# Attention and expert routing on one core: the order of a batch drawn up anew, long products halved, rank products joined, scatters one batch later

## What is computed

```python
# attention: 16 heads of width 8, all projected by U, V (8x8 here)
q, k, v = x @ Wq.T + bq, x @ Wk.T + bk, x @ Wv.T + bv       # per head, then @ V
att = softmax((q @ V) @ (k @ V).T / sqrt(rank))
y   = ((att @ (v @ V)) @ U.T) @ Wo.T + bo
x1  = layernorm(x + y)
# experts: 8 experts of hidden width 512, the best two per token
scores, idx = top_k(softmax(x1 @ gate_w.T), 2)              # scores normalised to sum 1
h   = relu(x1 @ w1[e].T + b1[e]);  out_e = h @ w2[e].T + b2[e]
out = layernorm(x1 + sum_e combine[e] * out_e)
```

## Time and profile before

| | us |
|---|---|
| median of 3 runs | 1183.03 (1179.2 to 1183.96) |
| the profiled execution | 1178.9 |
| its span in the trace | 1177.1 |
| PE / DVE / ACT / POOL busy | 1031.5 / 970.8 / 882.7 / 587.4 |
| first scores of batch 0, last scores of batch 15 | 63.9, 827.8 |
| first transpose of the second phase | 867.9 |

### The profile page before, as it was taken

One profiled execution on the slowest core, in us unless ns is written; L12 is line 12 of the kernel. 1 busy time (PEld: TensorE's weight loads), 2 busy tenths in 40 slices (PEclk: granted clock), 3 DMA queues, 4 the chain that ended last, 5 costly groups with the idle time before them and its releaser, 6 DMA issues. The chain is left out here.

```text
span 1177.1 us, 24412 instructions
## 1 busy us (share of the span) xinstructions
PE 1031.5 (88%) x7581; PEld 495.2 (42%) x7581; DVE 970.8 (82%) x2115; ACT 882.7 (75%) x1129; POOL 587.4 (50%) x823
## 2 busy tenths in 40 slices
PE   3578989999999999998999999897349999999967
PEld 1112223222222222222322222222249999999952
DVE  4778898999989989899899998991458888888845
ACT  1057878788788787887878878778259999999927
POOL 1223417346264372652734626314347777777745
PEclk9879999999999999999999999998669999999989
DMA  3633232241322423324224132200022222222246
GB/s 85 242 101 92 63 102 72 82 132 49 107 79 76 134 61 96 97 68 118 75 82 127 53 107 73 78 13 20 19 74 70 68 69 69 70 69 69 66 184 253
DMA packets 96420, 104.86 MB, mean 89 GB/s; under 512 B 21696, under 2 KB 73666, under 8 KB 96208
## 3 DMA queue, kind: packets, MB, share of 16 engines
q1 hardware_dynamic: 85872, 81.88, 24.0%
q0 software_dynamic: 8448, 16.93, 4.6%
q10 hardware_dynamic: 2016, 4.98, 1.2%
HBM read 56.06 MB, written 47.39 MB: 88 GB/s over the span
## 5 line engine op out<-in xcount | busy, mean ns | idle before, releaser
L753 DVE TENSOR_REDUCE row_max<-score_ps 128x2 f32<-128x1024 f32 x512 | 618.0, 1221 | 70.8 <-PE score_ps L552 68.1
L639 ACT ACTIVATE probs<-score_ps 128x1024 f32<-128x1024 f32 x512 | 521.3, 1022 | 134.2 <-PE score_ps L534 112.8
L800 POOL DMA_INDIRECT routed_d<-rows,slot_i x128 | 126.4, 988 | 318.7 <-DVE slot_i L722 272.2
L515 PE MATMUL av_ps<-probs,v_one 128*9 128x512 f32 x2048 | 271.0, 601 | 6.1 <-ACT probs L639 5.2
L552 PE MATMUL score_ps<-k_stack,q_stack 48*128 48x512 bf16 x1024 | 202.5, 392 | 54.7 <-ACT probs L639 26.4
L534 PE MATMUL score_ps<-q_stack,k_stack 51*128 51x512 bf16 x1024 | 201.4, 391 | 25.0 <-DVE row_max L753 20.8
L1058 ACT ACTIVATE w_cur<-experts 128x1156 f32 x136 | 158.4, 1167 | 38.0 <-issue 18.3
L534 PEld LDWEIGHTS score_ps<-q_stack,k_stack 51*128 51x128 bf16 x1024 | 49.2, 93 | 313.4 <-issue 161.2
L1154 POOL DMA_INDIRECT y_d<-y_out,place x136 | 136.8, 1006 | 44.8 <-issue 44.8
L1015 PE MATMUL up_ps<-xt_sb,w_cur 128*128 128x128 f32 x1088 | 145.5, 277 | 0.0
L1023 PE MATMUL down_ps<-w_cur,hidden_r 128*128 128x128 f32 x1088 | 143.4, 275 | 0.0
(11 more groups left out here) (171 smaller groups left out, 1050.8 us busy)
## 6 DMA issues: line engine op xcount, KB each, us to landing
k_stack<-k_stack_d SPq DMA_DIRECT2D x128, 96.0 KB, 2.5
q_stack<-q_stack_d SPq DMA_DIRECT2D x128, 96.0 KB, 2.6
x_rows_sb<-routed_d SPq DMA_DIRECT2D x136, 65.0 KB
q_stack_d<-q_parts SPq DMA_DIRECT2D x32, 192.0 KB
k_stack_d<-k_parts SPq DMA_DIRECT2D x30, 192.0 KB
experts<-expert_rows SPq DMA_DIRECT2D x1, 4624.0 KB, 15.1
x_t<-x_cols SPq DMA_DIRECT2D x16, 256.0 KB, 4.0
q_stack_d<-q_parts SPq DMA_DIRECT2D x32, 128.0 KB
```

The source lines that it names most:

```text
L515: last = nc.tensor.matmul(av_ps[32 * g:32 * g + V_COLS, :], v_one[n.parity][:, kb, HG * hg + g, :], probs[:, (2 * j + g // 2) % P_RING, g ...
L639: nc.scalar.activation(probs[:, s % P_RING, :, :], exp_bank(b, s)[:, :, :], ACT.Exp).then_inc(S["exp_done"], 1)
L753: nc.vector.tensor_reduce(row_max[:, m // (STEPS // 2), :, m % (STEPS // 2)], max_bank(b, s)[:, :, :], AX.X, ALU.max).then_inc(S["red_done ...
L800: nc.gpsimd.indirect_dma_start(routed_d, bass.IndirectOffsetOnAxis(ap=slot_i[n.parity][:, w, t:t + 1], axis=0), rows[n.parity][:, w, t, :] ...
```

## The change

- The pieces of `misc` get other steps. Before, every piece stands in an odd step. Now the y transposes stand at steps 14, 22, 0 (of the next batch) and 5, the rank at 24, the row maxima at 9 and 26, x1 at 28, the logits at 30.
- The long products are cut in two: q at steps 2 and 3 (before 13), k at 16 and 17 (before 15), the output product at 11 and 12 (before 11), v at 19 and 20 (before 19).
- The ranks come from 5 matmuls of 40, 32, 24, 16 and 8 columns instead of 14 of 8; `chosen_any` has a column block of zeros more.
- DVE gets one piece of `choose` a step (`CHOOSE_AT`), for batch b-2 and a batch later than before; `route` at 25 to 28; the sum, statistics and moments of the layer norm in three steps (13, 14, 16) instead of two.
- ACT's copies move to the steps behind their products; the scaling of x1 goes to steps 20, 22, 24, 26.
- POOL scatters batch b-3 in the body of b, two after every split; the last two batches' scatters come at the end. SP's order has q stores ahead of the second maxima rows, and `x_t` at the end of a body instead of the start of the next, which is the same place in its queue.

```diff
-SCALE_AT = 17
+SCALE_AT = (20, 22, 24, 26)
+CHOOSE_AT = (2, 3, 4, 5, 7, 8, 9, 10, 11, 12, 17, 18, 19, 20, 21, 22)
+ROUTE_AT = (25, 25, 26, 27, 28)
...
-                            if s == 13 and proj:
-                                pe.wait_ge(x_loaded[n2.parity], n2.count_parity(16, 16))
-                                emptied(s)
-                                nc.tensor.matmul(misc_ps[:, :], wq_t[:, :], x_t[n2.parity][:, :], start=True, stop=True).then_inc(S["q_done"], 1)
+                            if s in (2, 3) and proj:
+                                if s == 2:
+                                    pe.wait_ge(x_loaded[n2.parity], n2.count_parity(16, 16))
+                                    emptied(s)
+                                at = slice((s - 2) * T // 2, (s - 1) * T // 2)
+                                last = nc.tensor.matmul(misc_ps[:, at], wq_t[:, :], x_t[n2.parity][:, at], start=True, stop=True)
+                                if s == 3:
+                                    last.then_inc(S["q_done"], 1)
...
-                            if s == 17 and cur:
+                            if s == 14 and cur:
                                 emptied(s)
                                 y_transpose(b, 0)
...
-                            if s == 5 and prev2:
+                            if s == 24 and prev2:
                                 emptied(s)
                                 pe.wait_ge(S["top_step"], p2.count(TOP_STEPS, 13))
...
+                                counts = misc_ps[:, 0:(QT + 1) * E].rearrange("p (t e) -> p t e", e=E)
+                                nc.tensor.matmul(counts, before[:, :], chosen_any[p2.parity][:, :, :], start=True, stop=False)
+                                for k in range(QT):
+                                    last = nc.tensor.matmul(counts[:, k + 1:QT + 1, :], ones[:, :],
+                                                            chosen_any[p2.parity][:, k:k + 1, :].to_broadcast([P, QT - k, E]), start=False, stop=(k == QT - 1))
...
-                            if s <= 4 and prev2:
-                                for k in (2 * s + 6, 2 * s + 7):
-                                    choose(p2, k)
+                            if s in CHOOSE_AT and prev2:
+                                choose(p2, CHOOSE_AT.index(s))
...
+                        if nxt and n1.c + 2 < B:
+                            n3 = n1 + 2
+                            sp.wait_ge(S["v_done"], n1.count(1, 1))
+                            sp.dma_start(x_t[n3.parity][:, :], x_cols[n3.c, :, :]).then_inc(x_loaded[n3.parity], 16)
```

More of the change, by code:

```diff
@@ L172, in build_layer @@
             weight_sum = asb("weight_sum", [P, QT])
-            chosen_any = [asb(f"chosen_any{n}", [P, QT, E], bf16) for n in range(2)]
+            chosen_any = [asb(f"chosen_any{n}", [P, QT + 1, E], bf16) for n in range(2)]
             slot = asb("slot", [P, QT, E])
@@ L444, in misc @@
                                 max_transpose(1)
-                            if s == 11 and prev:
-                                pe.wait_ge(S["ynt_sb"], p1.count(1, 1))
-                                emptied(s)
-                                for t in range(QT):
+                            if s in (11, 12) and prev:
+                                if s == 11:
+                                    pe.wait_ge(S["ynt_sb"], p1.count(1, 1))
+                                    emptied(s)
+                                for t in (2 * s - 22, 2 * s - 21):
@@ new lines, in misc @@
+                            if s in (19, 20) and nxt:
+                                if s == 19:
+                                    pe.wait_ge(x_loaded[n1.parity], n1.count_parity(16, 16))
+                                    emptied(s)
+                                for t in (2 * s - 38, 2 * s - 37):
+                                    last = nc.tensor.matmul(misc_ps[:, t * P:(t + 1) * P], x_t[n1.parity][:, t * P:(t + 1) * P], wv_t[:, :], start=True, stop=True)
+                                if s == 20:
+                                    last.then_inc(S["v_done"], 1)
@@ L456, in misc @@
+                            if s == 22 and cur:
                                 emptied(s)
[L457 to L458 removed]
+                                y_transpose(b, 1)
+                            if s == 24 and prev2:
                                 emptied(s)
                                 pe.wait_ge(S["top_step"], p2.count(TOP_STEPS, 13))
[L461 to L468 removed]
@@ L469, in misc @@
-                            if s == 19 and nxt:
-                                pe.wait_ge(x_loaded[n1.parity], n1.count_parity(16, 16))
-                                emptied(s)
-                                for t in range(QT):
-                                    last = nc.tensor.matmul(misc_ps[:, t * P:(t + 1) * P], x_t[n1.parity][:, t * P:(t + 1) * P], wv_t[:, :], start=True, stop=True)
-                                last.then_inc(S["v_done"], 1)
-                            if s == 21 and cur:
-                                emptied(s)
-                                y_transpose(b, 1)
@@ L802, in scatter, with rows_ready @@
                                     rows[n.parity][:, w, t, :], None).then_inc(scattered[n.parity], 16)
[L804 to L807 removed]
+                        def rows_ready(n):
+                            pool.wait_ge(S["place_out"], n.count(1, 1))
+                            pool.wait_ge(S["top_step"], n.count(TOP_STEPS, TOP_STEPS))
+                            pool.wait_ge(S["slot_step"], n.count(SLOT_STEPS, SLOT_STEPS))
+                            pool.wait_ge(S["x1_ready"], n.count(QT, QT))
+                        if prev3 and cur:
+                            rows_ready(p3)
+                            scatter(p3, 0, 2)
                         if prev:
@@ L873, in stacks @@
                                                  stack_d[n.parity][a, :, :, pairs, :].rearrange("s r c t -> (s r) c t")).then_inc(stack_loaded[hg], 16)
-                        if cur and proj:
-                            sp.wait_ge(S["v_done"], b.count(1, 1))
-                            sp.dma_start(x_t[n2.parity][:, :], x_cols[n2.c, :, :]).then_inc(x_loaded[n2.parity], 16)
                         if nxt:
@@ L888, in body @@
                             store_parts(sp, q_stack_d[n2.parity], q_parts, Q_PLACES)
-                        if nxt and not cur:
-                            max_rows(n1, 0)
+                        if cur:
+                            max_rows(b, 1)
                         if proj and not is_first(b):
```

182 lines of the change are left out of this document (88 added, 94 removed).

## The result

The changed kernel takes **1301.7 us**, median of 4 runs (1296.42 to 1303.11). Beside it the kernel before took 1181.12 (4 runs, 1178.34 to 1183.96). The ratio is **1.1028**, 95% interval 1.1008 to 1.1048: slower by a tenth. The forecast was 1285 us, 1236 to 1330, and slower with a chance of 0.91.

A forecast was written before the change was run, and what follows sets the result against it. It took a loop of odd scores, exponential, even maxima and `av`, 2.81 us a pair, to bound the kernel. Terms summed to +101.6 on the profiled 1178.9, giving 1280.5, plus 4.1 for the median: 1285 us, range 1236 to 1330.

The forecast's parts named there:

- The rule: Pair costs 2.81 us, plus odd-step excess over 0.75, all PE work behind even `av`, 0.19 per last-moment ACT copy.
- A: PE products now behind `av` in even steps (transposes, half products, logits, row maxima, ranks) add their time: +88.9 us.
- B: ACT copies: v and x1 ahead of odd exponentials +5.7, three y copies beside PE products −8.2; together −2.5 us.
- C: The five long products lose their excess in odd steps: −22.7 us.
- D: DVE pieces, spread one a step, heal a leftover of 0.53 us in 14 batches: −7.4 us.
- E: PE's q product at step 2 waits 2.8 us for the load of `x_t` in 13 batches: +36.4 us.
- F: Maxima rows land late for the scores of step 16, 0.3 us in 13 batches: +3.9 us, bounds 0 and 9.
- G: Start: q product of batch 2 waits for `x_t` in batch 0, at lower clock: +3.5 us, bounds 0 and 8.
- H: End: scatters of batches 13 and 14 follow the last attention step: +1.5 us, bounds 0 and 3.
- The clock rival: TensorE's clock falls to 0.50 in each batch's wait for `x_t`: 42 us more, 1327 us; chance 0.18.
- The rival of the engines' sums: Pairs shift work freely, so a batch costs what its busiest engine, DVE, needs: 1140 us; chance 0.07.
- `x_t` in time: At step 2 the load of `x_t` comes in time, so PE does not wait: 1247 us; chance 0.14.

The follow-up runs named there:

- x8: Changed kernel with the `x_t` load early and ranks, maxima, x1 transpose and logits at odd steps 23, 25, 27, 29: 1220.55 us, ratio 1.0336.
- x1: Kernel before, with every product of `misc` and its copies and VectorE pieces one step later, in even steps: 1333.55 us, ratio 1.1304.
- x4: Changed kernel with the four long products uncut in odd steps (q 3, output 11, k 17, v 19): 1267.49 us, ratio 1.0740.
- x5: Changed kernel with the `choose` pieces laid two to a step again: 1312.07 us, ratio 1.109.
- x3: Changed kernel with the `x_t` load issued ahead of the maxima rows and the twelve stack loads: 1260.48 us, ratio 1.0702.
- x6: Changed kernel with `x_t` early, long products whole in odd steps, and batch 13's last scatters ahead of the last layer norm: 1234.82 us, ratio 1.0479.

## Why the prediction was right, and where its sizes were off

The sign, the range and the loop of the pairs held; the clock did not stay at 1.00, which the forecast had named as a sign that it was wrong. Its likeliest case was some 17 us short of the median, or 22 of the span's 124; that the median came 5 us nearer than the span is luck, since the forecast had added 4.1 for what the median takes over the profiled execution, and this time it took 1.4 less. By its own terms, where 64 + 46 + 1.6 + 7.3 make 119 of the 124:

- **A to D, the pairs: forecast +56.3, about +64 by the pairs.** The 13 pairs from (5, 6) to (29, 30) sum to 42.39 us, before 39.15, so +3.24 a batch; the three around the start of a batch, without wait and clock fall (as `x8` has them: 3.44, 2.81, 3.49), to 9.74 instead of 8.71, +1.03. 4.27 × 15 = 64. The rule gives 41.9 for the 13. (13, 14) at 3.40 and (29, 30) at 3.96 came as forecast (3.40, 3.99).
  - The failed size in A is the half product: 0.64, not half of 1.06 to 1.09. Three cut products show 3.45, 3.53 and 3.45 where the rule had 3.36, 3.34 and 3.36.
  - B held for the changed kernel, whose copies do not meet; `x1` shows that two of them ahead of an odd exponential cost twice.
  - C is what the cut was for, 22.7 us. It is repaid more than once by the even halves; `x4` shows the product whole in an odd step as the cheaper form.
  - D was expected to heal −7.4. It did not: the pairs (7, 8) and (23, 24) still have 0.1 over the rule, and `x5` moved pieces back with no effect on the pairs. DVE's busy time did not fall by 10 to 20 us, it rose by 14.7 us; I did not follow that up, since DVE ends none of these pairs.
- **E, the wait for x_t: forecast +36.4, in 13 batches.** As a wait it is 20.0 in 13 batches, 1.5 each instead of 2.8, and 3.0 in batch 0. From the row maxima at 445.45 to the issue at 457.61 went 12.2 us (12.6 estimated), the landing took 3.6 instead of 4.0, and in six of the 13 batches the clock's fall had already delayed PE. Yet what the start of a batch costs beyond the pairs is 13.05 − 9.74 = 3.3 us, 46 in 14 batches: the wait, and the clock that the forecast left to a rival. The load's place is worth 41 us by `x3`.
- **F, maxima rows for step 16: forecast +3.9.** Nothing here: waits for the rows are 1.5 us in the whole phase (before 2.4). With the wait for `x_t` gone they do come: in `x3` PE waits 4.5 us for them at step 16, in seven batches.
- **G, start: forecast +3.5.** Batch 0 took 57.6 instead of 48.4, 9.2 more, where the mean batch took 7.6 more; the excess of 1.6 is what G measures.
- **H, end: forecast +1.5, its upper bound 3.** It is 7.3: the step missed that the scaling of batch 15 writes the rows that the scatters of batch 13 read, and that these were put behind the layer norm. `x6` took 6.5 of it back.

**The clock rival was half of the truth.** The forecast said it would be wrong if the clock in the middle were under 1.00, and it was 0.97. The clock did fall, about once a batch, but a fall costs 1.6 us, not 3.2, since the level returns within one to two pairs (by 411 us, above). Nor is the wait for the load what it needs: with no such wait it fell at step 0 of every second batch (`x3`), behind the pairs (27, 28) and (29, 30), and it was gone with these two pairs short again (`x8`). The Trainium skill, TensorE: Matmul & The Clock Gate, tells of two forms: in the section on HAM oscillation, tiles that begin with a wait for a load, which the prediction weighed, and in the section behind it, on a second failure mode, an engine that idles briefly and often between groups of products while it goes round PSUM banks, which it passed over. The traces have falls that look like either: seven right behind the wait (408.80), the others ahead of it (454.95) or, in `x3`, without one (536.03, behind idle gaps of 0.68, 0.85 and 0.77). `x1` has four more without a wait for a load, at step 30, with all its pieces in even steps. What it is in these pairs that drops the clock, the runs don't settle.

**The rival of the engines' sums** fell: PE's and DVE's busy shares went down, not the time. `x_t` in time fell with the waits in all batches but one; with the load moved (`x3`) the kernel still stood at 1260, 13 above the 1247 of that case. Three sizes were too small there: six falls of the clock, 10 us, A to D by 8 and the drain by some 5. Together they are more than the 13, and I can't name what came out smaller.

## What to carry to other kernels

Where two engines hand one buffer to and fro, find the loop's pair of steps that has nothing else in it, and price each piece by which side of the hand-over it stands on: here the same transpose costs 0.00 us ahead of it, where it fills the 0.68 in which the engine would stand idle, and 0.59 behind it, where that idle time stays. Evening out pieces per step or cutting long ones helps only inside the covered side. When a consumer is moved up, move its load up in the issuing queue as well; `x_t` had a free place nine us earlier, and leaving it where it was cost 41 us.

## What the runs showed of the hardware that was not expected

- A half product, two or four matmuls, costs PE 0.64 us from its start to the next instruction's (422.16 to 422.80), a whole one 1.06 to 1.09: two halves cost about 0.2 more than the whole.
- TensorE's granted clock fell from 1.00 to 0.50 behind steps in which PE's idle gaps were 0.68, 0.85 and 0.77 us and nothing waited for a DMA, in strict turn, every second batch, 105.8 us apart (`x3`). One fall cost 1.6 us.
- Six DMA issues of maxima rows and twelve of stacks take SP 9.5 us before it comes to `x_t`, more than twice the 3.6 us that the data of `x_t` needs to land. The place in a queue decided, not the transfer.
